# Mixture-of-experts stage: another order of the weight parts in a tile, and two jobs of the first tiles moved to GpSimd

## The reference, cut to what matters

```python
logits = xf @ gate_W.T
pi = _sinkhorn(-logits)
_, top_idx = jax.lax.top_k(pi, TOP_K)              # TOP_K = 2
g = jnp.einsum('nd,efd->enf', xf, W_gate)          # E = 8, F = 1024, D = 256
u = jnp.einsum('nd,efd->enf', xf, W_up)
y = jnp.einsum('enf,edf->end', jax.nn.silu(g) * u, W_down)
for k in range(TOP_K):
    out = out + y[top_idx[:, k], n_ar] * pi[:, k:k + 1]
```

## Time and profile before

| | |
|---|---|
| median of 3 runs | 2107.75 us (2105.91 to 2108.53) |
| the profiled execution's own time | 2104.67 us |
| its span, first to last instruction | 2102.4 us |
| mean granted clock of TensorE | 0.949 |
| stage of the experts, about | 720 to 1386 us of the span |

### The profile page before, as it was taken

The page is one execution under the profiler, slowest core; times in us unless marked ns, Lnnn a source line. Parts: engine busy times, 40 slices in busy tenths (PEclk is TensorE's granted clock), DMA queues, the critical chain, the costliest instruction groups (busy, mean ns, idle before and its releaser), DMA issues. The chain is left out here.

```text
span 2102.4 us, 37210 instructions
## 1 busy us (share of the span) xinstructions
PE 1893.3 (90%) x11671; PEld 1072.3 (51%) x11671; DVE 1332.9 (63%) x2223; ACT 1386.7 (66%) x1586; POOL 706.3 (34%) x696
## 2 busy tenths in 40 slices
PE   6989999999956589999999999949899999999898
PEld 5822333333332478888878888847522222222255
DVE  4511135345667756565565656437599999999967
ACT  5689999999933223233233333227699999999934
POOL 2000111111110212222222122111188888898922
PEclk9999999999965599999999999979899999999999
DMA  6744334434210474555555555459935344364012
GB/s 200 250 100 71 46 76 91 90 71 90 54 42 0 160 246 160 205 181 194 184 187 182 180 196 172 158 200 347 254 60 127 61 76 113 46 159 61 24 68 72
DMA packets 133132, 276.06 MB, mean 131 GB/s; under 512 B 18732, under 2 KB 69166, under 8 KB 132104
## 3 DMA queue, kind: packets, MB, share of 16 engines
q1 hardware_dynamic: 119256, 231.86, 40.4%
q10 hardware_dynamic: 6848, 22.94, 3.4%
q0 software_dynamic: 6816, 18.62, 2.6%
HBM read 365.58 MB, written 96.21 MB: 220 GB/s over the span
## 5 line engine op out<-in xcount | busy, mean ns | idle before, releaser
L1326 PE MATMUL psum<-A_qa,A_ka 50*128 50x512 f32 x2048 | 408.2, 467 | 23.2 <-DVE A_qa L1413 6.2
L1326 PEld LDWEIGHTS psum<-A_qa,A_ka 50*128 50x128 f32 x2048 | 176.6, 185 | 471.6 <-DVE A1f_probs L1423 243.6
L2714 PE MATMUL psum<-e_w_high,e_xT 128*128 x1136 | 377.2, 404 | 28.0 <-issue 28.0
L1547 POOL TENSOR_TENSOR A1f_probs<-A1f_probs,A1f_bias 128x512 f32<-128x512 f32 x256 | 327.5, 1291 | 82.5 <-ACT A1f_probs L1378 82.0
L1423 DVE SCALAR_TENSOR_TENSOR A1f_probs<-psum,A1f_bias 128x1024 f32<-128x1024 f32 x256 | 311.7, 1218 | 23.7 <-PE psum L1326 20.2
L1378 ACT ACTIVATE A0f_probs<-psum 128x1024 f32<-128x1024 f32 x256 | 316.3, 1236 | 0.0
L1366 ACT ACTIVATE A0f_probs<-psum 128x1024 f32<-128x1024 f32 x256 | 314.0, 1226 | 2.5 <-PE psum L1326 2.4
L1345 PE MATMUL psum<-A1f_probs,v 128*32 128x512 f32 x2048 | 274.2, 606 | 17.5 <-POOL A1f_probs L1547 16.4
L1370 ACT ACTIVATE A1f_probs<-A1f_probs 128x1024 f32<-128x1024 f32 x256 | 273.9, 1070 | 4.8 <-DVE A1f_probs L1423 3.9
L1345 PE MATMUL psum<-A0f_probs,v 128*32 128x512 f32 x2048 | 273.5, 606 | 0.0
L1378 ACT ACTIVATE A1f_probs<-psum 128x1024 f32<-128x1024 f32 x256 | 263.7, 1030 | 0.0
(11 more groups left out here) (308 smaller groups left out, 2534.1 us busy)
## 6 DMA issues: line engine op xcount, KB each, us to landing
e_w_raw<-in_experts ACTq DMA_DIRECT2D x67, 2048.0 KB
e_w_raw<-in_experts ACTq DMA_DIRECT2D x67, 1024.0 KB
hidden<-e_squares SPq DMA_DIRECT2D x69, 512.0 KB, 3.3
e_turned<-hidden SPq DMA_DIRECT2D x276, 128.0 KB, 2.7
qk_parts<-L_part SPq DMA_DIRECT2D x64, 512.0 KB, 4.4
A_qa<-qk_parts SPq DMA_DIRECT2D x192, 128.0 KB, 4.4
A_ka<-qk_parts SPq DMA_DIRECT2D x192, 128.0 KB, 6.6
om<-results SPq DMA_DIRECT2D x16, 512.0 KB, 6.9
```

The source lines that it names most:

```text
L1326: mm = e.matmul(ps[:, side * HALF:(side + 1) * HALF], self.qk.ka[rows, s, pair, kt * P:(kt + 1) * P].bitcast(FP32R), self.qk.qa[rows, s, p ...
L1547: e.tensor_tensor(fourth, fourth, self.bias_of(*w[1:], slice(self.FOURTH, GH)).rearrange("p h q -> p (h q)"), ALU.mult).then_inc(self.mult ...
L2714: mm = e.matmul(out, left[part].bitcast(FP32R), moving.bitcast(FP32R), start=start and i == 0, stop=stop and i == 2)
```

## The change

Four things are edited.

1. DVE's order in a tile: the down part of tile j-3 goes from the head of the tile (after `rest_of_hidden`, before `split_rows`) to its end (after `square` and the gate part).
2. ACT's order: the high down part is that of tile j-3 and comes right after silu and the high up part, no longer that of tile j-2 behind `move_y`. The two conditional fetches come after it and before `move_y`; the one of down is of tile j-4, no longer j-3. Flags are read ahead of the waits.
3. PE waits for the gate part of tile j-2 before the gate product, and for the up part of tile j-2 only before the up product. It reads `buffer_of` and `is_new` before it waits, and has one more branch on `is_new` in tiles 3 to 5.
4. The low part of the second expert is made on GpSimd, in six subtractions of 1024 columns, at its tile 0 (`low_of_second`), and the fourth expert's fetch is one DMA of 3 MB issued by GpSimd behind it. `low_second`, `low_rest` and SP's `fetch_up` are gone. A semaphore `first_low` with value 4 tells PE.

```diff
 # DVE, tile j
-            if j == 1:
-                low_second()
             if j >= self.LAG:
                 rest_of_hidden(j - self.LAG)
-            if j == 3:
-                low_rest(DOWN_AT, WIDE)
-            if j > self.LAG:
-                low_part(j - self.LAG, "down", DOWN_AT, WIDE)
             if j + 1 < MOE_TILES:
                 split_rows(j + 1)
-            if j == 2:
-                low_rest(DC * F, DOWN_AT)
             if j > 1:
                 low_part(j - 1, "up", DC * F, DOWN_AT)
...
             if 1 <= j < self.LAST:
                 low_part(j, "gate", 0, DC * F)
-            if j == 1:
-                low_rest(0, DC * F)
+            if j > self.LAG:
+                low_part(j - self.LAG, "down", DOWN_AT, WIDE)
 # ACT, tile j, after silu
             if 1 <= j < self.LAST:
                 e.wait_ge(self.upped, j)
                 high_part(j, "up", 0, DOWN_AT)
+            if j > self.LAG:
+                high_part(j - self.LAG, "down", DOWN_AT, WIDE)
+            if j > self.LAG + 1:
+                e.wait_ge(self.low_ready, self.low_value("down", j - self.LAG - 1))
+                self.fetch_next(e, flags, j - self.LAG - 1, (DOWN_AT, WIDE), self.second_in)
             if 1 <= j - 1 <= self.LAST_FETCH:
                 e.wait_ge(self.low_ready, self.low_value("up", j - 1))
                 self.fetch_next(e, flags, j - 1, (0, DOWN_AT), self.weights_in)
...
             if j >= self.LAG:
                 move_y(j - self.LAG)
-                high_part(j - self.LAG + 1, "down", DOWN_AT, WIDE)
-            if j > self.LAG:
-                e.wait_ge(self.low_ready, self.low_value("down", j - self.LAG))
-                self.fetch_next(e, flags, j - self.LAG, (DOWN_AT, WIDE), self.second_in)
 # PE
         def wait_for_weights(j):
+            buffer_of(j)
+            is_new(j)
+            if j < self.SECOND_BY:
+                with e.If(is_new(j) > 0):
+                    e.wait_ge(self.first_low, self.SECOND_LOW)
+            elif j == self.SECOND_BY:
+                e.wait_ge(self.first_low, self.SECOND_LOW)
             if j > self.REST:
-                e.wait_ge(self.low_ready, self.low_value("up", j - 2))
-            else:
-                with e.If(is_new(j) > 0):
-                    e.wait_ge(self.low_ready, self.low_value("second", 1) if j == 1 else self.low_value("rest", 2))
+                e.wait_ge(self.low_ready, self.low_value("gate", j - 2))
...
+            if j > self.REST:
+                e.wait_ge(self.low_ready, self.low_value("up", j - 2))
             up_product(j, 1)
 # GpSimd
+    def low_of_second(self, e):
+        e.wait_ge(self.first_low, self.SECOND_LOW - 1)
+        for k in range(1, self.REST + 1):
+            with self.if_second(e, k):
+                e.wait_ge(self.high_ready, self.high_value("second", k))
+                for at in range(0, WIDE, F):
+                    raw, high, low = (x[:, 0, at:at + F] for x in (self.w.raw, self.w.high, self.w.low))
+                    e.tensor_tensor(low.bitcast(FP32R), raw, high, ALU.subtract)
+        e.drain().then_inc(self.first_low, 1)
+        e.wait_ge(self.first_low, self.SECOND_LOW)
+        self.fetch(e, 0, FOURTH, (0, WIDE), self.fourth_in)
...
             if j >= self.LAG:
                 self.store_y(e, j - self.LAG)
+            if j == 0:
+                self.low_of_second(e)
```

## The result

The changed kernel takes 2078.99 us (median of 4 runs, 2074.71 to 2080.32) beside 2108.14 us for the kernel before on the same chip: a ratio of 0.9858, 95% interval 0.9841 to 0.9876. The forecast was 2063.4 us in a range of 2057 to 2076. The direction was right; 29 us came where 44 were forecast. The profiled execution took 2080.32 us, which is 24.35 less than that of before, and the trace says where these lie.

The account below looks back on a forecast made before the run. PE, busy 90% of the span, was taken as the bound, losing time to holes and lowered clock. New experts -38.2 us and first tiles -6.2 made -44.4: 2060.3 profiled, plus 3.1 for the median, 2063.4 us, range 2057 to 2076.

Parts of the forecast that it names:

- Order of DVE and ACT: At new experts, moving the down part, high part and down fetch removes B and C at no added cost.
- B: PE idle 0.49 us in tile 14 ahead of the down product, for tile 11's low hidden values; forecast to go.
- C: PE idle 1.52 us ahead of tile 15's gate product, behind DVE's low down part; forecast to go, clock loss too.
- Split wait: PE at new experts: the later up-part wait removes A, leaving 0.2 us per new expert, 1.4 in all.
- A: PE idle 1.54 us ahead of tile 13's gate product, waiting for tile 11's low up part; forecast to go.
- Second expert's low part: First tiles: moving it off DVE saves 9.2 us, less 1.0 for PE's branch and 2.0 for GpSimd's queue: -6.2 us.
- (c): Tiles 0 and 1: GpSimd's subtractions slow DVE's operations with two SBUF inputs; +0 us (0 to 2.7).
- (d): GpSimd's queue: 3 MB fetch and gather of row tile 7 behind the subtractions delay PE at tile 6, +2.0 us.
- (e): SP loses waits and 3 MB ahead of its squares, so tile 2's squares get out sooner; no effect on time.
- Half given back: New experts: late down part or ACT chain leaves holes, about 2.4 us each, 17 in all: 2079 us; 15% chance.
- GpSimd becomes the start's bound: First tiles: slow fetch, rows for tile 7 at 776 or later, +7 instead of +2: 2071 us; 13% chance.
- Slower: Every tile: PE's wait between gate and up product shows sequencer time, 1.0 us per tile giving 2131 us; 3% chance.

Follow-up runs that it names:

- e3: The changed kernel with two of ACT's flag reads (OTHER_BUFFER, FOURTH) moved from ahead of the high part to behind it: 2073.26 us, ratio 0.9832.
- e9: The changed kernel with PE's reads of buffer and new-flag behind the wait again, split wait kept: 2077.62 us, ratio 0.9851.
- e7: The changed kernel with PE waiting for the up part ahead of the gate product again, early reads kept: 2075.96 us, ratio 0.9860.
- e10: The changed kernel with both parts of PE's edit undone, one wait and reads behind it: 2096.32 us, ratio 0.9938.
- e6: The changed kernel with ACT's two flag reads behind the high part and the fourth expert's 3 MB fetch at GpSimd's tile 8: 2064.08 us, ratio 0.9800.
- e12: The kernel of e6 with the fourth expert's fetch in three 1 MB parts at GpSimd's tiles 4, 5 and 6: 2064.61 us, ratio 0.9793.
- e8: The kernel of e6 with GpSimd's six subtractions of 1024 columns cut into 24 of 256: 2064.79 us, ratio 0.9802.

## Why the prediction came out as it did

*Order of DVE and ACT (edits 1 and 2): right as to B and C, one cost missed.* Both holes went, and the clock loss with them: tiles 6 to 68 run at 1.00. The step that failed is "Flags and branches issued per tile are as many as before". As many they are, but three reads stand ahead of the high part now, where one did: two more, 1.1 us on ACT (1.40 less the 0.30 of e3). e3 shows 5.4 us of excess for them, of the 11.1 by which the new experts missed.

*Split wait (edit 3): A went, but the reason given is only one of two.* The prediction had the price right, "the time until PE's sequencer has got through its registers and branch", 1.95 us, and then credited the later wait with the cure. e9 shows that this would have done, e7 that the two lines ahead of the wait do it as well, and e10 that one of the two is needed. The prediction doesn't speak of those two lines. The 0.2 us left for a new expert are 1.8 in the profile (13.7 less the 1.2 us by which the other tiles were over 8.555 in the kernel before, by seven). About 0.8 of it is the flags. The rest, with the hole of 0.55 us ahead of tile 13's gate product, is not settled: that hole stands in e7 (0.71) and e9 (0.56) as well, so neither of PE's edits alone made it; what it likely is stands above.

*Second expert's low part (edit 4): the terms for DVE, PE and GpSimd were about right.* Tiles 2 and 3 lost 8.2 us for 8.2 forecast, by terms that were partly off both ways (nothing seen there of the 1.0 us for the branch, but the hole of 1.09). Tile 4 has a hole of 1.02 us ahead of its gate product; whether it is the branch or late hidden values is open. The six subtractions took 15.17 us for 16.0, ended at 757.1 for 755.5 to 758, and the fetch was issued at 759.18. By the Trainium skill's GPSIMD Engine Reference, section 3, the estimate was 13.5 us; the trace is slower. (c) had +0 (0 to 2.7) for the turns; the trace has a hole of 1.09 us in tile 3.

*Term (d), the collision, was put on the wrong transfer.* It named the gather of row tile 7, at +2.0 us. In the trace of the changed kernel no hole comes from rows. In that of e9 there is one of 2.34 us for them at tile 6's head, so the mechanism exists, at the size given:

```profile
772.50 0.44 PE L2734 MATMUL psum<-ident,e_x 128*128 128x128 f32 x2 [2.34 <-DMA e_x<-token_rows,tokens]
```

The step that failed is (e): "tile 2's squares get out sooner. Nothing, as PE does not wait for them now". Their loads had 5.5 us to spare, which I never worked out, and took 13, as the fetch, 14.4 us long, was issued 2.2 us ahead of them. That is 8 us of hole and, with the clock at 0.81, 9.7 us over a plain tile. By the Trainium skill (DMA: Bandwidth & Descriptors, SWDGE path) the estimate for the fetch was 9.2 us, and (d) nothing; the trace has 14.4.

*The rivals.* "Half given back" has the right number, 2079, by luck: it had 17 us lost to a late down part in tile 14, and there is no hole there. "GpSimd becomes the start's bound" is the nearest in mechanism, +7 us at the start, but by squares, not rows. "Slower" did not come: by e7 against the changed kernel (0.9860 and 0.9858) a wait in the middle of each tile costs nothing that can be measured.

With both failed steps mended the kernel takes 2064.1 (e6) or 2064.6 us (e12), where 2063.4 was forecast. That it is so near is partly luck: e6 still has 10.0 us of excess, where the forecast had 2.6 (its 1.4 and the 1.2 of the other tiles). Its tiles 1 to 5, 39.9 us, are 1.8 under the forecast, which has 2.0 for a collision that e6 doesn't have, and its median isn't 3.1 above its profiled execution's time.

## What to carry to other kernels

When a large transfer is moved, list every small one that will run beside it, with its issue, its usual landing and its due time; what has a few microseconds to spare is the next hole. Here cutting the large one in three spaced parts was as good as moving it away. A wait costs also what its engine must read and branch on between it and the first instruction: put reads ahead of a wait that is held, and behind the work when the wait is not. A count of instructions that stays the same says nothing as long as their place in the order changes.

## What the runs showed of the hardware

- With two reads of a table and a branch behind a held wait, PE goes on 1.95 us after the awaited work ends; with the reads ahead of the wait, 0.65 us (e10, e7). Two more such reads take ACT 1.1 us (1.40 in the changed kernel, 0.30 in e3).
- A fetch of 3 MB issued by GpSimd took 14.4 us, and 14.6 in e6; four loads of 128 KB issued 2.2 us behind it took 13 us, where 0.50 MB of such loads had moved in the 3 us behind 749.3.
- GpSimd's subtraction of 1024 columns took 2.53 us, and DVE's operation with two inputs in SBUF (`rest_of_hidden`) took up to 2.2 us longer beside pieces of 2.53 us and 0.63 beside pieces of 0.78 (e8), as if it waited for the piece in hand. The section Who interferes with whom of the Trainium skill's page SBUF — State Buffer says that a DVE instruction with two SBUF inputs contends with a GpSimd instruction that reads SBUF, and that this contention is an exclusive lock. The 3.42 us for 1.23 agree.
